# The last seven of 39 expert tiles hold 64 rows instead of 128, in a fused attention and mixture-of-experts kernel

## What is computed

```
xn = layernorm(x)
attention: q, k, v = xn @ Wq[h] + bq[h], ...    (16 heads of 16)
           softmax(q k^T * 0.25 + causal) v, then @ Wo + bo
experts:   logits = xn @ Wr; the best two of 8, softmax over the two
           for each expert e: (clip(silu(xn @ Wg[e])) * (xn @ Wu[e])) @ Wd[e], times its weight
out = x + attention + experts
```

## Time and profile before

| | before |
|---|---|
| median of 3 runs (lowest, highest) | 438.08 us (437.95, 439.42) |
| profiled execution | 438.36 us |
| its span, first to last instruction | 436.4 us |
| TensorE busy | 412.3 us (94%) |
| VectorE busy | 332.0 us (76%) |
| ScalarE busy | 222.4 us (51%) |
| GpSimd busy | 196.5 us (45%) |
| mean granted TensorE clock | 0.978 of 2.4 GHz |

### The profile page before, as it was taken

How to read it: one execution, slowest core, us unless ns; L and a number is a source line. 1 busy time by engine, 2 the same in 40 slices (tenths; PEclk the granted TensorE clock), 3 DMA queues, 4 the chain that set the end, 5 groups by cost and what they waited for, 6 DMA issues and landing times.

```text
span 436.4 us, 8151 instructions
## 1 busy us (share of the span) xinstructions
PE 412.3 (94%) x2755; PEld 246.4 (56%) x2755; DVE 332.0 (76%) x1043; ACT 222.4 (51%) x511; POOL 196.5 (45%) x223
## 2 busy tenths in 40 slices
PE   8998979989999999999799999999999999999993
PEld 8585414655364465566547567565667476556332
DVE  6827999999989859775287866789396988881795
ACT  1563362334646566545164355456555445646970
POOL 5331266576064187256474265415655255313320
PEclk9999979999999999999899999999999999999996
DMA  7289896788067089235954239805595336110782
GB/s 228 82 218 194 289 200 211 226 285 282 3 160 174 1 252 279 75 110 170 214 168 156 103 110 249 248 24 182 164 235 178 136 101 194 24 26 6 236 271 72
DMA packets 40372, 71.33 MB, mean 163 GB/s; under 512 B 5893, under 2 KB 30598, under 8 KB 40332
## 3 DMA queue, kind: packets, MB, share of 16 engines
q0 software_dynamic: 9360, 39.99, 29.1%
q1 hardware_dynamic: 27132, 26.76, 25.0%
q10 hardware_dynamic: 3840, 4.08, 3.7%
HBM read 55.85 MB, written 15.60 MB: 164 GB/s over the span
## 4 chain that ended last, share of the span: by engine, by line
PE 68%; DVE 21%; DMA 4%; issue 4%; ACT 1%; POOL 1%; SPq 0%; ACTq 0%; DVEq 0%; POOLq 0%
PE psum L1293 14%; PE psum L1330 14%; PE psum L1254 11%; PE psum L1273 11%; PE psum L1339 8%; DVE psum L981 7%; DVE mxa L984 4%; PE psum L1209 3%; PE psum L1185 3%; PE psum L1312 3%; DMA bqk<-in_bqk 2%; PE psum L1320 2%; DMA xg<-xn_rows,token 2%; DVE resid L953 1%; DMA x<-in_x 1%
## 5 line engine op out<-in xcount | busy, mean ns | idle before, releaser
L894 ACT ACTIVATE probs<-psum 128x512 f32<-128x512 f32 (+1 forms) x320 | 151.1, 581 | 40.9 <-PE psum L1273 40.3
L981 DVE CUSTOM_DVE_ANT_0 psum<-psum,maskrow 128x128 f32<-128x128 f32 (+3 forms) x256 | 121.4, 506 | 14.3 <-PE psum L1254 14.0
L1254 PE MATMUL psum<-packk,packq 96*128 96x512 bf16 (+3 forms) x384 | 94.2, 328 | 3.3 <-DVE mxb L981 1.2
L1273 PE MATMUL psum<-packq,packk 99*128 99x512 bf16 (+3 forms) x384 | 91.0, 330 | 3.3 <-ACT probs L894 2.1
L984 DVE TENSOR_REDUCE mxa<-psum 128x1 f32<-128x512 f32 x128 | 87.7, 685 | 5.4 <-PE psum L1254 5.3
L1293 PE MATMUL psum<-probs,v 128*32 128x512 f32 (+3 forms) x768 | 75.7, 503 | 1.0 <-POOL probs L821 0.9
L1254 PEld LDWEIGHTS psum<-packk,packq 96*128 96x128 bf16 x384 | 35.1, 97 | 56.1 <-issue 15.9
L821 POOL TENSOR_SCALAR_AFFINE_SELECT probs<-probs 128x512 f32<-128x512 f32 (+1 forms) x48 | 41.2, 863 | 44.8 <-ACT probs L894 44.7
L1273 PEld LDWEIGHTS psum<-packq,packk 99*128 99x128 bf16 x384 | 33.4, 98 | 42.7 <-issue 10.5
L788 POOL DMA_INDIRECT xg<-xn_rows,token x39 | 37.7, 967 | 38.9 <-PE psum L1320 27.4
L806 POOL DMA_INDIRECT expert_rows<-wvr,slots x39 | 39.3, 1008 | 31.8 <-ACT wvr L914 17.2
(11 more groups left out here) (120 smaller groups left out, 457.8 us busy)
## 6 DMA issues: line engine op xcount, KB each, us to landing
qk_parts<-stage SPq DMA_DIRECT2D x24, 256.0 KB, 3.9
stage<-expert_rows SPq DMA_DIRECT2D x16, 256.0 KB, 4.1
packq<-qk_parts SPq DMA_DIRECT2D x16, 192.0 KB, 5.4
packk<-qk_parts SPq DMA_DIRECT2D x14, 192.0 KB, 5.8
x<-in_x SPq DMA_DIRECT2D x4, 512.0 KB, 6.2
packq<-qk_parts SPq DMA_DIRECT2D x16, 128.0 KB, 6.0
xn_rows<-probs ACTq DMA_DIRECT2D x4, 512.0 KB, 14.7
out<-x SPq DMA_DIRECT2D x16, 128.0 KB, 3.0
```

What stands on the lines that cost most here:

```text
L894: act.activation(probs[:, g % RING, h, 0:width], psum[:, bank, 0:width], ACT.Exp, scale=SCALE)\
L981: ins = dve.tensor_tensor_reduce(out=chunk, in0=chunk, in1=maskrow[:, BANK - width:], scale=1.0, scalar=NEG, op0=ALU.add, op1=ALU.max, acc ...
L1254: pe.matmul(psum[:, bank, 0:width], packq[0:MAXROW, u % SLOTS, i // HALF, h, P * (i % HALF):P * (i % HALF + 1)], packk[0:MAXROW, u % SLOTS ...
L1273: ins = pe.matmul(psum[:, bank, at:at + width], packk[0:KROWS, u % SLOTS, j // HALF, h, P * (j % HALF):P * (j % HALF + 1)], packq[0:KROWS, ...
```

## The change

The number of tiles stays 39. The first 32 keep 128 rows and the last 7 hold 64. The pairs of an expert are cut into units of 64. Two units make a full tile; an odd last unit goes to a half tile. If the full tiles come to more than 32, the surplus spills to half tiles too. For the half tiles, gather, scatter, `copy_xgt`, the two operations of `copy_yo` and tanh, `hidden`, and the moving side of `gate_up` take 64 rows; `transpose_rows` and `down` are unchanged. `place_slots` and `tile_experts` have more steps, and the planner's costs follow. The new function `by_rows` cuts a tile's columns.

```diff
+FULL_TILES = 2 * N // P
+MAX_TILES = FULL_TILES + E - 1
+HALF_ROWS = P // 2
+def tile_rows(i):
+    return P if i < FULL_TILES else HALF_ROWS
...
-    dve(("place",), 3700, [("PE", ("route",))], 20003, frees=("route",))
+    dve(("place",), 6500, [("PE", ("route",))], 20003, frees=("route",))
...
-    dve(("experts",), 1600, [("DVE", ("tiles", 1))], 20005)
+    dve(("experts",), 2900, [("DVE", ("tiles", 1))], 20005)
...
-        pe(("gu", i), 1850, [("ACT", ("xgt", i)), ("POOL", ("fetch", i))], due + 500, ("gu", i))
+        pe(("gu", i), 1850 * part, [("ACT", ("xgt", i)), ("POOL", ("fetch", i))], due + 500, ("gu", i))
...
+        def by_rows(cols, i):
+            return cols if tile_rows(i) == P else cols.rearrange("p (m t) -> p m t", t=P)[:, :, 0:tile_rows(i)]
...  place_slots
+                chain(route_step, dve.tensor_tensor(
+                    fits[:, :, :, :], psum[:, bank, P:P + E].unsqueeze(1).unsqueeze(3).to_broadcast([P, 2, E, NT]),
+                    iota128[:, :, :].unsqueeze(2).to_broadcast([P, 2, E, NT]), ALU.is_gt))
+                chain(route_step, dve.tensor_reduce(ntile[:, :, :], fits[:, :, :, :], op=ALU.add, axis=AX.X))
+                chain(route_step, dve.tensor_tensor(ntile[:, 0, :], ntile[:, 0, :], ntile[:, 1, :], ALU.subtract))
+                for k in range(2):
+                    ins = dve.tensor_tensor_scan(tend[:, k, :], one8[:, :], ntile[:, k, :], 0.0, ALU.mult, ALU.add)
+                ins.then_inc(tend_ready, 1)
                 dve.wait_ge(tend_ready, 1)
+                dve.tensor_scalar(spill[:, 0:1], tend[:, 0, E - 1:E], float(P), -float(2 * N), ALU.mult, ALU.add)
+                dve.tensor_scalar(spill[:, 1:2], tend[:, 0, E - 1:E], float(FULL_TILES), None, ALU.add)
+                dve.tensor_scalar(edge[:, :], ntile[:, 1, :], float(P), None, ALU.mult)
+                chain(route_step, dve.tensor_tensor(sbase[:, :, :], tend[:, :, :], ntile[:, :, :], ALU.subtract))
+                chain(route_step, dve.tensor_scalar(wrap[:, :], sbase[:, 0, :], float(E - 1), -float(E), ALU.is_ge, ALU.mult))
+                chain(route_step, dve.tensor_tensor(wrap[:, :], wrap[:, :], sbase[:, 0, :], ALU.add))
+                chain(route_step, dve.tensor_tensor(moved[:, :], wrap[:, :], tend[:, 1, :], ALU.subtract))
+                dve.tensor_scalar(moved[:, :], moved[:, :], float(P), -float(2 * N), ALU.mult, ALU.add)
+                chain(route_step, dve.tensor_tensor(late[:, :, :], rank, by_token(edge[:, :]), ALU.is_ge))
+                dve.scalar_tensor_tensor(place[:, :, :], by_token(sbase[:, 1, :]), float(P), rank, ALU.mult, ALU.add)
+                chain(route_step, dve.tensor_tensor(late[:, :, :], late[:, :, :], by_token(moved[:, :]), ALU.mult))
+                chain(route_step, dve.tensor_tensor(place[:, :, :], place[:, :, :], late[:, :, :], ALU.add))
...
                 chain(route_step, dve.tensor_copy(posi[:, :, :], posf[:, :, :]))
+                chain(route_step, dve.tensor_scalar(postile[:, :, :], posi[:, :, :], -HALF_ROWS, None, ALU.bitwise_and))
+                chain(route_step, dve.tensor_scalar(over[:, :, :], postile[:, :, :], spill[:, 0:1], None, ALU.add))
+                chain(route_step, dve.scalar_tensor_tensor(over[:, :, :], posf[:, :, :], float(2 * N), over[:, :, :],
+                                                           ALU.is_ge, ALU.mult))
+                chain(route_step, dve.tensor_tensor(posf[:, :, :], posf[:, :, :], over[:, :, :], ALU.add))
+                chain(route_step, dve.tensor_copy(posi[:, :, :], posf[:, :, :]))
...  tile_experts
+                dve.tensor_scalar(halves_end[:, 0, :], tend[:, 0, :], float(FULL_TILES), None, ALU.add)
+                chain(route_step, dve.tensor_scalar(halves_end[:, 1, :], tend[:, 1, :], 2.0, -float(2 * FULL_TILES), ALU.mult, ALU.add))
+                chain(route_step, dve.tensor_scalar(halves_end[:, 1, :], halves_end[:, 1, :], 0.0, spill[:, 1:2], ALU.max, ALU.add))
+                dve.tensor_tensor(below[:, 0:FULL_TILES, :], *tiles_from(0, FULL_TILES, tend[:, 1, :]))
+                dve.tensor_tensor(split[:, :, :], *tiles_from(FULL_TILES, MAX_TILES, halves_end[:, 0, :]))
+                chain(route_step, dve.tensor_tensor(below[:, halves, :], *tiles_from(FULL_TILES, MAX_TILES, halves_end[:, 1, :])))
+                dve.tensor_reduce(nsplit[:, :], split[:, :, :], op=ALU.add, axis=AX.X)
                 chain(route_step, dve.tensor_reduce(eidf[:, :], below[:, :, :], op=ALU.add, axis=AX.X))
+                chain(route_step, dve.scalar_tensor_tensor(nsplit[:, :], split[:, :, E - 1], -float(E), nsplit[:, :], ALU.mult, ALU.add))
+                chain(route_step, dve.tensor_tensor(eidf[:, halves], eidf[:, halves], nsplit[:, :], ALU.add))
...  gate_up
-                        ins = pe.matmul(psum[:, bank, P * m:P * (m + 1)], wexp[i % WSLOTS][:, at:at + P], xgt[:, i % 2, c, :],
+                        ins = pe.matmul(psum[:, bank, P * m:P * m + tile_rows(i)], wexp[i % WSLOTS][:, at:at + P],
+                                        xgt[:, i % 2, c, 0:tile_rows(i)],
```

More of the change, by code:

```diff
@@ L414, in make_plan @@
             after += [("PE", ("x", i - 2))]
-        job("POOL", ("gather", i), 1250, after, due - 8000, lag=2200, size=131072)
+        job("POOL", ("gather", i), 1250 if part == 1 else 1000, after, due - 8000, lag=2200, size=131072)
         after = [("DVE", ("experts",)), ("PE", ("list",))] + ([("PE", ("d", i - WSLOTS))] if i >= WSLOTS else [])
@@ L528, in build @@
         hots = sb("hots", [P, NT, E], BF16)
-        fits = sb("fits", [P, E, NT])
-        ntile = sb("ntile", [P, E])
-        tend = sb("tend", [P, E])
+        ntile = sb("ntile", [P, 2, E])
+        tend = sb("tend", [P, 2, E])
         one8 = sb("one8", [P, E])
-        sbase = sb("sbase", [P, E])
+        sbase = sb("sbase", [P, 2, E])
+        wrap = sb("wrap", [P, E])
+        moved = sb("moved", [P, E])
+        edge = sb("edge", [P, E])
+        spill = sb("spill", [P, 2])
+        late = sb("late", [P, NT, E])
         place = sb("place", [P, NT, E])
         prod = sb("prod", [P, 2, NT, E])
+        fits = prod[:, :, :, :].rearrange("p k t e -> p (k t e)").rearrange("p (k e t) -> p k e t", k=2, t=NT)
         posf = sb("posf", [P, 2, NT])
+        over = sb("over", [P, 2, NT])
         posi = sb("posi", [P, 2, NT], I32)
@@ L787, in gather @@
                     wait_filled(pool, ("x", i - 2))
-                pool.indirect_dma_start(out=xg[:, i % 2, :], out_offset=None, in_=xn_d,
-                                        in_offset=bass.IndirectOffsetOnAxis(ap=token[:, i:i + 1], axis=0))\
+                rows = tile_rows(i)
+                pool.indirect_dma_start(out=xg[0:rows, i % 2, :], out_offset=None, in_=xn_d,
+                                        in_offset=bass.IndirectOffsetOnAxis(ap=token[0:rows, i:i + 1], axis=0))\
                     .then_inc(gather_in[i % 2], 16)
@@ L805, in scatter @@
                 wait_freed(pool, ("d", i))
[L806 to L807 removed]
+                rows = tile_rows(i)
+                pool.indirect_dma_start(out=z_d, out_offset=bass.IndirectOffsetOnAxis(ap=slots[0:rows, i:i + 1], axis=0),
+                                        in_=yo[0:rows, i % 2, :], in_offset=None, bounds_check=2 * N - 1, oob_is_err=False)\
                     .then_inc(scatter_out[i % 2], 16)
@@ L1086, in place_slots, with by_token @@
-                dve.wait_ge(tend_ready, 1)
[L1087 to L1090, removed]
+                rank = psum[:, bank, 0:P].rearrange("p (t e) -> p t e", e=E)
+                def by_token(t):
+                    return t.unsqueeze(1).to_broadcast([P, NT, E])
```

45 lines of the change are left out of this document (25 added, 20 removed).

## The result

The changed kernel is slower, by about 11 us: a median of 449.11 us (447.7 to 452.42, 4 runs) against 438.19 us before, ratio 1.0254 with a 95% interval of 1.0195 to 1.0314. A second set of its runs beside the experiments gave 1.0244 (1.0196 to 1.0291). The prediction had 441.6 us and a range up to 446.

The account below looks back on a forecast made before the run. VectorE was taken to bound the kernel before 107 us, TensorE after. 438.36 us profiled + 3.9 for added VectorE steps - 0.4 for gate and up = 441.9, or 441.6 us as a median; range 435 to 446 us.

Parts of the forecast that it names:

- What bounds: Whole kernel: VectorE's work is on the path before 107 us, TensorE's work counts after it.
- One after another: Chain of waits from 42.3 to 107.5 us: said to be made of VectorE pieces, each following the last.
- Part 1: Gate and up of seven half tiles: weight loads keep the pace, so halved moving columns save only 0.4 us.
- the first rival: Gate and up matmuls run at half, saving 6.0 us, and VectorE's addition is half hidden: 434.5 us; chance 0.12.
- Parts 2 and 3: VectorE's added steps before 107 us: placing 3.65 us longer, experts' list 1.27 us longer, together 4.9 us.
- The contention: VectorE's placing beside GpSimd's subtraction: one added step may wait 0.8 us more, or a waiting one may not.
- What they cost: VectorE's added 4.9 us before 107 us: four fifths, 3.9 us, reach the path; ends 1.5 and 4.9 us.
- the switch: Where the chain goes over from VectorE to TensorE: expected at about 111 us rather than 107.5.
- The fourth rival: Longer placing starves TensorE, so the half clock lasts another stretch, 3.4 us more: 445.0 us; chance 0.16.
- The second rival: Load sets gate and up's pace, but VectorE's addition is hidden by TensorE's queue: 439.2 us; chance 0.18.
- Part 5: Planner's order from 50 us on, reshuffled by new costs: taken as 0, with a 5 us hole gone or added.
- the third rival: As forecast, but the hole at 212 us before L1320 is gone, 5 us less: 436.6 us; chance 0.12.

Follow-up runs that it names:

- the gap filled: Changed kernel's work in the order of before, 40 identity transposes put ahead of the first three score products where TensorE starves: 443.35 us, ratio 1.0118.
- The order's two parts: Kernel before with only planner costs changed: placing and experts' list in one run, 444.52 us, ratio 1.0136; half tiles' costs in another, 441.59 us, ratio 1.0077.

## Why the prediction was right and wrong

**What bounds: right in the main.** "One after another" was too much. The chain also holds 5.5 us that aren't VectorE's, between 82.8 and 88.3 us: a gate and up product of 1.89, six matmuls of L1185 in 2.59 and a copy on ScalarE of 0.70, with a score product of 0.23 ahead of them.

**Part 1, gate and up: right.** A saving of 0.4 us was expected; measured is between 0.35 us less and 1.0 more (0.9992 to 1.0023 of 438 us), so no saving is shown and 0.4 lies at the edge. The mechanism holds: the step stays at 0.112 us, and the first rival, which had 6 us, is out. The Trainium skill ("TensorE: Matmul & The Clock Gate", section "LDWEIGHTS (loading the stationary operand)") has a load's time go by its columns alone; by that rule 107 and 53 ns, and the runs' 112 and 58 ns agree. The isolated gap by moving columns, which the prediction took from the Trainium skill's same page (section "Back-to-back issue gap"), would be 29 ns for 64 columns. The measured step is 112 ns, and the section itself says that this formula counts too little at few columns, since it has no load in it. So it was a weak ground for the first rival.

**Parts 2 and 3, the steps on VectorE: right.** 3.65 and 1.27 us expected, 3.36 (7.07 less 3.71) and 1.26 (2.61 less 1.35) measured. The contention stayed at one step.

**What they cost: right in kind, too small, and only in the order of before.** Four fifths of 4.9 us, 3.9, were to reach the path. With the order of before 5.6 us did (interval 3.4 to 7.8), by the switch 5.96. I had bounded it above by the added work itself. But up to the switch VectorE is not only busy for 4.1 us more, it is idle for 1.8 us more. Of that 1.2 us goes with TensorE's low clock (3.71 us idle, 2.50 with the gap filled). My reading is that TensorE, starved and slow, hands VectorE its scores late; what the rest is isn't shown. The fourth rival's 3.4 us for a longer half clock is refuted in this order, where filling the gap gained at most about 1.3. In the changed kernel's own order it is untested. The second rival (addition hidden) is out for the order of before. In the new order the addition does not show at all (448.63 us with it, 449.24 without).

**Part 5, the order: this step failed.** "I take 0" for a new order, with plus or minus one hole of 5 us as the bound, was the error, and by itself larger than everything else in the sum. The changed order costs 5.2 us over that of before with the new work (448.63 less 443.4), and 11.3 us by the ratio when the work is the old one, some 2 of which may be the late start. I had named late transfers as the danger, but looked only at the hole there was, 3.26 us before L1320. That one did go, as the third rival said (TensorE is idle for 0.77 us between 200 and 220 us, where it was for 3.26). But the new order made others. A scatter goes out at 133.84 us, and ScalarE's copy two tiles on, which waits for it, comes up before it has landed and stands ahead of the exponentials. A second such wait follows near 279 us. Six buffers take the waits away and 6.1 us with them. The planner reckons 3.1 us from the start of a scatter to its landing (1.3 for the issue and 1.8 behind it); here it was 7.5.

The account of the 11 us: 6.1 go with the wait for late scatters, and the order made that wait. With it gone, the new order is no slower than the old one with the same work (1.0105 and 1.0128). Some 4.6 us are left. With the order of before the added VectorE steps would account for them, but in the new order no run parts the steps, the order of the first phase and the low clock: new order, old work and six buffers weren't run together. So "5.6 for the work and 5.2 for the order" is the split for the work taken first; with the order taken first it is 11.3 and about nothing. The order's two parts, 1.0136 and 1.0077, sum to 1.0213 and not to 1.0259. That is within the intervals, and the late start of 2.0 us (0.5%) would fill it.

Why that scatter took 7.5 us is read from the trace alone. Twelve pack loads were issued beside it (129.94 to 137.20 us), and so were two fetches of an expert's weights, which go out through GpSimd as the scatter does: one at 132.57 us, just ahead of it, which landed after 8.2 us, and one at 135.15. No run parts the two.

## What to carry to other kernels

Before shrinking the moving side of a float32 matmul, compare it with the weight load beside it: here 128 columns in the load and 128 moving ones took about the same time, so cutting the moving side alone brought nothing, and only cutting both did (0.058 for 0.112 us). Where the order is computed from costs, a change of any cost is a change of the whole kernel: run the new costs with the old work, and the new work with the old costs, before either is believed, and don't expect the two to add. And where an engine's in-order list waits for a transfer's landing, provide buffers for the late landings and not for the mean one (here up to 10 us for a median of 4), since everything behind the wait in that list is held up.

## What the runs showed of the hardware that I had not expected

A float32 matmul's listed duration didn't tell its stream: 275 ns with 64 moving columns and 280 with 128 while the load had 128 columns, and 228 ns once the load had 64. The spacing of loads told it (0.112 and 0.058 us). An indirect scatter of 128 rows of 1 KB took 7.5 us to land beside twelve pack loads and two fetches of weights; over the whole run such scatters took 2.0 to 10.5 us, at a median of 4.5. Raising TensorE's granted clock from 0.90 to 0.97 in a phase that VectorE paces changed the time by nothing that can be seen (ratio 1.0118 for 1.0128).
